# A recommender layer in split fp32r: the low part of each weight piece made in four VectorE steps instead of two

## What is computed

```python
sparse_embed = emb_tables[field_idx[None, :], x_sparse]      # 512 x 26 x 64
z = sparse_embed.reshape(B, 26 * 64)
gram = jnp.einsum('bik,bjk->bij', sparse_embed, sparse_embed)
inner = gram[:, iu, ju]                                       # 325 pairs, i < j
dnn_in = jnp.concatenate([x_dense, z, inner], axis=-1)        # 512 x 2002
h = jax.nn.relu(dnn_in @ w1 + b1)                             # w1: 2002 x 2002
out = jax.nn.sigmoid(h @ w2 + b2)                             # 512 x 1
```

## Time and profile before

| | us |
|---|---|
| median of three runs | 213.66 (212.72 to 214.28) |
| the profiled execution, its time | 214.66 |
| the profiled execution, its span | 212.5 |

### The profile page before, as it was taken

One profiled execution on the slowest core, in us unless ns is written; L12 is line 12 of the kernel. 1 busy time (PEld: TensorE's weight loads), 2 busy tenths in 40 slices (PEclk: granted clock), 3 DMA queues, 4 the chain that ended last, 5 costly groups with the idle time before them and its releaser, 6 DMA issues.

```text
span 212.5 us, 3900 instructions
## 1 busy us (share of the span) xinstructions
PE 201.6 (95%) x1340; PEld 161.4 (76%) x1340; DVE 148.6 (70%) x347; ACT 129.3 (61%) x256; POOL 129.4 (61%) x210
## 2 busy tenths in 40 slices
PE   8859999999999999999999799799999999999994
PEld 8834888877777878776887688588888877788882
DVE  3559457488937779879459796777587679773483
ACT  2657443479948939977338844679698558542201
POOL 4887888888787878218877878788788500000000
PEclk9997999999999999999999999999999999999999
DMA  5676999968484912326965667698975637223100
GB/s 153 188 226 201 305 327 344 323 203 281 119 291 125 299 51 63 86 56 169 325 217 178 196 180 189 185 329 299 325 213 161 207 98 212 87 35 63 32 0 0
DMA packets 15388, 39.00 MB, mean 184 GB/s; under 512 B 3881, under 2 KB 5281, under 8 KB 15369
## 3 DMA queue, kind: packets, MB, share of 16 engines
q1 hardware_dynamic: 11688, 35.27, 51.3%
q0 software_dynamic: 3328, 3.41, 7.6%
q10 hardware_dynamic: 353, 0.08, 0.2%
HBM read 37.71 MB, written 0.69 MB: 181 GB/s over the span
## 4 chain that ended last, share of the span: by engine, by line
PE 69%; POOL 15%; DMA 6%; issue 5%; DVE 3%; ACT 2%; DVEq 0%; POOLq 0%; ACTq 0%
PE slot L1079 20%; PE slot L1082 19%; PE slot L1085 19%; POOL E L823 13%; DMA E<-emb,row_idx 5%; PE slot L1039 4%; PE slot L1018 3%; POOL pace L831 2%; DVE G L977 2%; PE slot L1071 1%; PE slot L1069 1%; PE slot L1070 1%; ACT w_hi L847 1%; DMA x_idx<-idx 1%; DVE slot L1003 1%
## 5 line engine op out<-in xcount | busy, mean ns | idle before, releaser
L823 POOL DMA_INDIRECT E<-emb,row_idx x104 | 111.7, 1074 | 37.8 <-POOL pace L831 25.7
L929 DVE TENSOR_TENSOR w_lo<-w_raw,w_hi 128x500 fp32r<-128x500 f32 (+6 forms) x128 | 80.8, 671 | 13.2 <-ACT w_hi L847 12.5
L847 ACT CAST w_hi<-w_raw 128x1000 fp32r<-128x1000 f32 (+6 forms) x64 | 65.7, 1029 | 27.3 <-DMA w_raw<-w 15.4
L1079 PE MATMUL slot<-w_hi,x_hi 128*128 128x500 f32 (+5 forms) x236 | 75.0, 399 | 3.4 <-ACT x_hi L873 2.1
L1082 PE MATMUL slot<-w_lo,x_hi 128*128 128x500 f32 (+5 forms) x236 | 73.3, 390 | 2.3 <-DVE w_lo L929 2.2
L1085 PE MATMUL slot<-w_hi,x_lo 128*128 128x500 f32 (+5 forms) x236 | 72.7, 389 | 0.0
L1079 PEld LDWEIGHTS slot<-w_hi,x_hi 128*128 128x128 f32 (+2 forms) x236 | 43.0, 189 | 15.3 <-ACT x_hi L873 5.0
L1082 PEld LDWEIGHTS slot<-w_lo,x_hi 128*128 128x128 f32 (+2 forms) x236 | 44.5, 189 | 12.1 <-DVE w_lo L929 3.0
L1085 PEld LDWEIGHTS slot<-w_hi,x_lo 128*128 128x128 f32 (+2 forms) x236 | 44.4, 189 | 9.3 <-DVE x_lo L959 0.2
L878 ACT COPY ET<-T 32x128 f32<-32x128 f32 (+4 forms) x88 | 32.1, 364 | 2.0
L946 DVE STREAM_TRANSPOSE T<-E 128x256 f32<-128x256 f32 x24 | 10.6, 443 | 18.8 <-DMA E<-emb,row_idx 18.6
(11 more groups left out here) (39 smaller groups left out, 85.8 us busy)
## 6 DMA issues: line engine op xcount, KB each, us to landing
w_raw<-w SPq DMA_DIRECT2D x32, 501.0 KB, 4.7
w_raw<-w SPq DMA_DIRECT2D x32, 500.0 KB, 4.7
E<-emb,row_idx POOLq DMA_INDIRECT x104, 4.3
w_all<-w SPq DMA_DIRECT2D x1, 1001.0 KB, 6.9
gram_dram<-G SPq DMA_DIRECT2D x8, 84.5 KB
x_in<-gram_dram SPq DMA_DIRECT2D x8, 42.0 KB
x_in<-G SPq DMA_DIRECT2D x4, 58.5 KB
x_in<-G SPq DMA_DIRECT2D x4, 19.5 KB
```

The costliest lines, as they stand in the source:

```text
L823: nc.gpsimd.indirect_dma_start(out=E[:, k % ER, j, :], out_offset=None, in_=emb_rows, in_offset=bass.IndirectOffsetOnAxis(ap=row_idx[:, at ...
L847: nc.scalar.copy(w_parts(m)[0], w_source(m)).then_inc(w_hi_ready, 1)
L929: nc.vector.tensor_tensor(lo[:, cols], w_source(m)[:, cols], hi[:, cols].bitcast(F32), ALU.subtract)\
L1079: nc.tensor.matmul(acc[q], xh, hi[:, cols[q]], start=first, stop=False)
```

## The change

Each chunk of w_lo is made in two steps: the first 250 columns, and the rest (252 or 250). So a piece takes four steps (LO_STEPS), numbered 0 to 3, each of which adds 1 to w_split. TensorE's waits for the chunks are now for the second and the fourth step, the load of piece m waits for all four steps of piece m - 5. The planner takes four operations of 0.45 us where it took two of 0.70 us, and may put other operations between any two of them.

```diff
-DVE_LEN = {"lo": 0.70, "turn": 0.46, "x24": 0.60, "x_lo": 0.44, "evac": 0.38, "park": 0.70, "drain": 0.86}
+DVE_LEN = {"lo": 0.45, "turn": 0.46, "x24": 0.60, "x_lo": 0.44, "evac": 0.38, "park": 0.70, "drain": 0.86}
 HOP = 0.08
+LO_STEPS = 4
...
-                    if ("lo", m - RAW, 1) not in done:
+                    if ("lo", m - RAW, LO_STEPS - 1) not in done:
                         break
-                    at = max(at, done["lo", m - RAW, 1] + HOP)
+                    at = max(at, done["lo", m - RAW, LO_STEPS - 1] + HOP)
...
-            late = {("x_lo",) + key_of(s): X_LO_LATE, ("lo", m, 0): LO_LATE, ("lo", m, 1): LO_LATE + 0.22}
+            late = {("x_lo",) + key_of(s): X_LO_LATE, ("lo", m, 1): LO_LATE, ("lo", m, 3): LO_LATE + 0.22}
...
-            for q in (0, 1):
+            for q in range(LO_STEPS):
                 offer("dve", ("lo", op[1], q), end + HOP + 0.01 * q)
...
                     if m >= RAW:
-                        sp.wait_ge(w_split, 2 * (m - RAW + 1))
+                        sp.wait_ge(w_split, LO_STEPS * (m - RAW + 1))
...
-                    cols = CHUNK_COLS[PIECES[USED[m]][2]][q]
+                    chunk = CHUNK_COLS[PIECES[USED[m]][2]][q // 2]
+                    cut = chunk.start + 250
+                    cols = slice(cut, chunk.stop) if q % 2 else slice(chunk.start, cut)
                     nc.vector.tensor_tensor(lo[:, cols], w_source(m)[:, cols], hi[:, cols].bitcast(F32), ALU.subtract)\
                       .then_inc(w_split, 1)
...
                         for q in (0, 1):
-                            pe.wait_ge(w_split, 2 * RANK[n] + q + 1)
+                            pe.wait_ge(w_split, LO_STEPS * RANK[n] + 2 * q + 2)
```

## The result

The changed kernel takes **218.76 us** (median of four, 218.25 to 221.37) against 213.28 for the kernel before (median of four): ratio **1.027**, 95% interval 1.023 to 1.032. It is slower by 5.5 us, outside the range that was given. Ratios leave out executions that count as disturbed (on one core: more than 1.5% above the kernel's fastest); a mean in this text is one over all executions of a kernel. The profiled execution took 218.25 us, with a span of 216.3 against 212.5. It is the fastest of the four, and the profiled one of the kernel before (214.66) lies above all four of its own, so the two profiles hold only 3.8 of the 5.5 us.

A forecast was written before the change was run, and what follows sets the result against it. It took TensorE (busy 95%) as the bound, with GpSimd's gathers the path from 94 to 134.9 us. Gram stretch 0.1 plus orders 0.2 gave +0.3 on the median 213.66: 214.0 us, range 212.4 to 216.8.

The forecast's parts named there:

- The price of a step: On VectorE: a 250-column step costs 0.324 us in a row, 0.12 more a piece, 7.7 us in all.
- Steps pay in full: Rival, chance 0.06: four steps in a row cost VectorE 0.31 us a piece more; 214.3 us.
- The start: Near 13.8 us: a w_lo chunk is 0.1 us later, covered by the gathers' pace; 0 on the path.
- The Gram stretch: 68 to 94 us, TensorE dense: w_lo steps between VectorE's copies make the fourth Gram round later; 0.1 us.
- the Gram rounds slip: Rival, chance 0.26 including other orders holding TensorE as long: one or two products more ahead of round four; 215.4 or 216.7 us.
- The orders: Planner charges 1.92 us a piece instead of 1.46 and reorders: from 0.66 us gained to 2.73 lost; +0.2 taken.
- From 94 to 134.9 us the path is GpSimd: TensorE's 1.09 + 1.42 us of idle time there cover a w_lo that is 0.12 late; 0 on the path.
- the tail: After 134.9 us: w_lo runs ahead of the products; 0 on the path.
- What would show it wrong: Signs against the forecast: Gram rounds a product later, longer TensorE waits for w_lo, or a later end from stops behind 135 us.
- the sign as written: At the end: forecast wrong if the last product ends over 2 us later from stops behind 135 us.
- The sum of TensorE's waits for w_lo: Sign, on TensorE: forecast wrong if these waits exceed 5.2 us by more than 1 us in sum.

The follow-up runs named there:

- the steps alone: Kernel before, its orders kept, each w_lo step cut in two back to back: mean 218.3 us (ratio 1.023); later sets had means 217.6 and 219.1.
- memset: Kernel before with a 2-column memset behind each 500-column w_lo step: mean 213.2 us against 215.3.
- extra subtract: Kernel before with a 16-column subtract, waiting for its forerunner, behind each 500-column w_lo step: mean 214.0 us against 213.9 (ratio 1.000).
- x_hi moved: Kernel before with one x_hi on ScalarE put ahead of a w_hi cast that waits for a DMA: mean 214.0 us against 213.9.
- the charge alone: Kernel before, two steps a piece, with the planner's charge for a w_lo step at 0.93 instead of 0.70: mean 218.8 us (ratio 1.020).
- the waits ahead of every second step: Kernel before, w_lo steps cut in two, each chunk's first step waiting for the step before it: median 212.70 us, mean 212.9 (ratio 0.993).
- the mended orders: Changed kernel with operations moved at phase B's start, later transposes, a Gram round's copies and the last load: 218.9 us (ratio 1.018).
- all mended, whole chunks: Changed kernel's orders, mended in all those places, with each w_lo chunk made in one step: 219.0 us (ratio 1.023).

## Why the prediction was wrong

*The price of a step* was right: 409 ns (410 forecast), 1.39 to 1.41 us for a row of four (1.39), and 8.0 us more of VectorE's time with the steps alone (7.7). In the changed kernel the 7 to 9 us don't show, since the planner moved the copies, as the text had said it would. *Steps pay in full* falls with it.

*The start*: the piece at 13.8 us was to be 0.1 later. The gather landed earlier in this profile, and the stop is 0.73 us at 11.98 instead of 2.17; the product behind the matmuls of ones starts 2.8 earlier. The gathers' pace takes back only part of that: the pair at 67.91 starts at 66.22, 1.7 earlier. This isn't the change's doing: in the three later profiles with the order before and whole chunks (memset, extra subtract, x_hi moved) the product behind the matmuls of ones starts 3.1 to 3.2 us earlier than in the profile that the prediction read. One profile's start was taken for the kernel's.

*The Gram stretch*: +0.1 forecast, the fourth round at 92.8 to 93.2. It starts at 91.43, and in the same three profiles without the change at 91.76 to 92.09. Profiles differ by more than the term, so its sign isn't shown. The rival *the Gram rounds slip* didn't happen: the round stands behind 51 products, as before.

**The first failed step: "The orders ... The middle of what I think likely is much nearer to the first: +0.2", with the upper end at two products ahead of Gram round four, 2.73 us.** The changed kernel's mean is 5.9 us above before; with whole chunks its orders alone cost 5.9 us, and the charge alone 4.6. The bound was taken at one place, because the chain of the earlier trace rows enters GpSimd there. The harm came behind it, where the text had counted 1.09 + 1.42 us of TensorE's idle time as cover, and in the tail, which it had left at 0. That idle time isn't free: the same engines whose order changes feed it, and a stop there grew from 1.09 to 2.39 us, with the lower clock behind it. The working named the right mechanism, "it can slip a transpose between two steps of a chunk", and then priced it by what it could gain.

**The second: "From 94 to 134.9 us the path is GpSimd; ... On the path: 0."** Finding that GpSimd is the path was right; then the change was priced by what VectorE hands to TensorE and never by what VectorE does to GpSimd. The steps alone cost 3.7 to 4.6 us on the mean, in three sets of executions, and the waits ahead of every second step take the held gathers and this price away together. The row that could have warned stands in the trace before: gathers take 0.95 to 1.5 us depending on what VectorE does beside them, and one who asks what a change of VectorE does to the engine on the path would have listed them.

*What would show it wrong*: the last product ends 3.8 us later, but 1.85 of that stems from ahead of 135 us and 1.95 from behind, so the sign as written (over 2 us from stops behind 135 us) just missed; none of the signs covered 112 to 124 us. The sum of TensorE's waits for w_lo did not flag it: 5.8 us against 5.2, since the stops were for x_hi and copies.

How much of the changed kernel's time the short steps cost isn't shown. Its profile has four gathers above 1.6 us, so they are held there too, but its orders with whole chunks take no less (5.9 us above before, with no held gather), and the mended orders take 218.9 us with short steps and 219.0 without. So the orders by themselves can account for all of the change; the held gathers are a second price, shown in the order before. Which of the changed orders costs what stays open.

## What to carry to other kernels

If GpSimd's gathers are on the path, price every change of VectorE by what it does to them: lay the gathers' durations one by one beside VectorE's timeline, and don't cut VectorE's two-input steps into short ones back to back without measuring it. A planner's charge is part of the kernel: changing one figure of it moved the time by 4.6 us with nothing else in the program edited, and moving single operations back by hand didn't recover that. Take a change apart into instructions and order before explaining it, and give each part a dozen executions where the scatter is 2 us.

## What the runs showed of the hardware

- **The clock.** Behind some stops of TensorE (2.39 us in the changed kernel, 2.94 with the steps alone) groups of two matmuls start 0.83 us apart instead of 0.455, the lower of the two levels (1.2 instead of 2.4 GHz), and lose 1.5 us more in the changed kernel; behind others not (1.97 us at 134, with x_hi moved in the kernel before), while one of 1.50 us (all mended, whole chunks) has the lower level behind it. So a stop can cost more than its length, and its length alone doesn't say whether.
- The kernel with the steps alone scatters by 2.4 to 2.7 us (standard deviation of its three sets), the kernel with waits ahead of every second step by 1.4, the kernel before by 1.1 to 1.5 on the same chips.
